# Two LayerNorms in a row folded into one, and input and output moved by groups, in a twelve-stage fp32 network on one core

## The reference, cut to what matters

```python
def _layernorm(x, axis=-1, eps=1e-05):
    m = jnp.mean(x, axis=axis, keepdims=True)
    v = jnp.var(x, axis=axis, keepdims=True)
    return (x - m) / jnp.sqrt(v + eps)
...
x = x + 0.5 * _L1_ffn_ref(_layernorm(x, axis=-1), L1_ffn_weight, L1_ffn_ln_gamma, L1_ffn_ln_beta)
...
x = x + _L3_attn_ref(_layernorm(x, axis=-1), ...)
...
def _L1_ffn_ref(x, weight, ln_gamma, ln_beta):     # ffn1, the quantised stage
    mu = jnp.mean(x, axis=-1, keepdims=True)
    var = jnp.var(x, axis=-1, keepdims=True)
    xn = (x - mu) * jax.lax.rsqrt(var + 1e-3) * ln_gamma + ln_beta
    ...
    gamma = jnp.max(jnp.abs(xn))                   # over all tokens: nothing goes on before all are normalised
    xq = jnp.clip(xn * QB / gamma, -QB + EPS, QB - EPS)
    y = jnp.einsum('bsd,du->bsu', xq, w_q)
    return y * (gamma * beta / QB)

def _L3_attn_ref(x, ...):                          # attn3, 16 heads, relative positions
    mu = jnp.mean(x, axis=-1, keepdims=True)
    var = jnp.mean((x - mu) ** 2, axis=-1, keepdims=True)
    xn = (x - mu) * jax.lax.rsqrt(var + 1e-05) * ln_gamma + ln_beta
    ...
```

## Time and profile before

| what | before |
|---|---|
| median of 3 runs | 4579.53 us (4579.15 to 4584.91) |
| span of the profiled execution | 4582.6 us |
| PE busy, share of the span | 3971.2 us, 87% |
| VectorE busy | 3493.0 us, 76% |
| ScalarE busy | 3069.3 us, 67% |
| GpSimd busy | 1526.0 us, 33% |
| mean granted TensorE clock | 0.928 of full |

### The profile page before, as it was taken

The page is one execution under the profiler, slowest core; times in us unless marked ns, Lnnn a source line. Parts: engine busy times, 40 slices in busy tenths (PEclk is TensorE's granted clock), DMA queues, the critical chain, the costliest instruction groups (busy, mean ns, idle before and its releaser), DMA issues.

```text
span 4582.6 us, 66148 instructions
## 1 busy us (share of the span) xinstructions
PE 3971.2 (87%) x15980; PEld 2219.1 (48%) x15980; DVE 3493.0 (76%) x11277; ACT 3069.3 (67%) x5649; POOL 1526.0 (33%) x2846
## 2 busy tenths in 40 slices
PE   5688759999999999999999999994878549999965
PEld 4466624444444444444444444442555437777744
DVE  5898479888888788887887887885656956666678
ACT  3455338999899899998998998992222216666632
POOL 2322124444444444444443443443000014333310
PEclk8888769999999999999999999996999769999977
DMA  2122010000000000100000000000000001111100
GB/s 56 29 34 37 15 23 1 1 24 1 15 10 1 20 6 1 25 1 15 10 1 20 6 1 22 3 1 0 1 0 0 1 14 43 43 43 43 43 1 18
DMA packets 151432, 71.88 MB, mean 16 GB/s; under 512 B 109433, under 2 KB 141902, under 8 KB 151012
## 3 DMA queue, kind: packets, MB, share of 16 engines
q1 hardware_dynamic: 144612, 64.16, 5.6%
q10 hardware_dynamic: 6400, 3.15, 0.2%
HBM read 54.48 MB, written 12.80 MB: 15 GB/s over the span
## 4 chain that ended last, share of the span: by engine, by line
PE 55%; DVE 21%; ACT 12%; issue 8%; DMA 1%; POOL 1%; DVEq 0%; ACTq 0%; SPq 0%; POOLq 0%
PE bank L1877 19%; PE bank L1892 6%; PE bank L1921 5%; PE bank L2663 5%; PE bank L1931 3%; DVE arena L1324 2%; PE bank L2696 2%; DVE arena L1328 2%; PE bank L655 2%; ACT arena L1969 2%; ACT arena L1968 2%; ACT L2015 2%; ACT arena L1981 2%; ACT arena L1972 2%; PE bank L2723 1%
## 5 line engine op out<-in xcount | busy, mean ns | idle before, releaser
L1877 PE MATMUL bank<-arena 128*128 128x512 f32 x3072 | 1423.2, 596 | 12.6 <-DVE arena L2058 6.1
L1877 PEld LDWEIGHTS bank<-arena 128*128 128x128 f32 x3072 | 587.2, 191 | 758.7 <-issue 730.1
L2118 POOL TENSOR_SCALAR arena<-arena 128x256 f32<-128x256 f32 x1024 | 483.7, 483 | 1191.0 <-DVE arena L2051 1191.0
L1892 PE MATMUL bank<-arena 128*128 128x512 f32 x1024 | 526.6, 606 | 64.8 <-DVE arena L2081 64.4
L2040 DVE SCALAR_TENSOR_TENSOR arena<-arena 128x256 f32<-128x256 f32 x1024 | 393.9, 421 | 185.9 <-ACT arena L1969 178.1
L2081 DVE SCALAR_TENSOR_TENSOR arena<-arena 128x256 f32<-128x256 f32 x1024 | 493.5, 526 | 13.5 <-issue 12.4
L2058 DVE SCALAR_TENSOR_TENSOR arena<-bank,bv,arena 128x256 f32<-128x256 f32 x1024 | 445.1, 472 | 0.0
L1968 ACT ACTIVATE arena<-bank,bqk 128x512 f32<-128x512 f32 x512 | 348.3, 680 | 81.5 <-PE bank L1877 72.9
L2051 DVE SCALAR_TENSOR_TENSOR arena<-bank,bq,arena 128x512 f32<-128x512 f32 x512 | 384.3, 751 | 18.0
L1981 ACT ACTIVATE arena<-arena,const_table 128x512 f32<-128x512 f32 x512 | 374.5, 731 | 0.0
L1972 ACT ACTIVATE arena<-bank,bqk 128x512 f32<-128x512 f32 x512 | 354.1, 692 | 0.7 <-PE bank L1877 0.6
(11 more groups left out here) (370 smaller groups left out, 7497.0 us busy)
## 6 DMA issues: line engine op xcount, KB each, us to landing
arena<-packed_dram SPq DMA_DIRECT2D x96, 96.0 KB
arena<-packed_dram SPq DMA_DIRECT2D x32, 288.0 KB
arena<-diag_dram SPq DMA_DIRECT2D x16, 256.0 KB, 4.0
arena<-in_L_attn_Wk_dram SPq DMA_DIRECT2D x16, 256.0 KB, 3.3
arena<-in_L_attn_Wq_dram SPq DMA_DIRECT2D x16, 256.0 KB, 4.0
arena<-in_L_attn_Wv_dram SPq DMA_DIRECT2D x16, 256.0 KB, 4.5
arena<-in_L_attn_Wo_dram SPq DMA_DIRECT2D x8, 512.0 KB, 3.9
arena<-in_L_attn_W_dram SPq DMA_DIRECT2D x16, 256.0 KB, 2.8
```

The lines of the kernel that those rows point to most:

```text
L1877: nc.tensor.matmul(bank[:, RING1[m % 5], :], w1p[k][:, i * P:(i + 1) * P], zT_of(g), start=True, stop=True).then_inc(a1_proj.sem, 1)
L1892: nc.tensor.matmul(bank[:, 6, :], wo1[:, i, :], a1_att[:, i % 4, :], start=(i == 0), stop=(i == NB1 - 1)).then_inc(a1_outd.sem, 1)
L2118: last = nc.gpsimd.tensor_scalar(a, a, 1.0, a1_ksum[:, i % 4, b:b + 1], ALU.add, ALU.mult)
```

## The change

It has three parts.

1. The second LayerNorm is folded into the first. With variance v and the two constants e1 and e2, the normalised x has mean 0 and variance v/(v+e1), so that both together are (x-m) / sqrt((1+e2)v + e1 e2). `ln_steps` takes the second constant (`again`), and `rstd_pool` multiplies by a slope and adds an offset in the one tensor_scalar where it added eps and multiplied by 1. `second_ln` with its four steps, and its tiles and semaphores, are gone.
2. In ffn1 VectorE's pipeline is stats (lag 0), apply (1), max (2). In attn3 the stats stand at w = 6, rstd at w = 7 on GpSimd, and apply at w = 10.
3. The first group of x is loaded by a transfer of its own that ScalarE issues as its first instruction (`group_loaded`), and SyncE's transfer brings the other seven; VectorE waits for these in the statistics of group 1. At the end SyncE waits for each group of the last stage and stores it by itself, 8 transfers of 256 KB.

```diff
-        def second_ln(n, eps, rep, apply_scale=None):
...
-        def ln_steps(n, eps, src=None):
+        def ln_steps(n, eps, again=None):
+            slope, offset = (1.0, eps) if again is None else (1.0 + again, eps * again)
...
             def stats_dve(g, u):
                 if n:
                     x_written.wait(nc.vector, t(g) - G)
+                elif isinstance(g, int) and g == 1:
+                    nc.vector.wait_ge(loaded, 16)
...
-                nc.gpsimd.tensor_scalar(rstd[:, u, :], meanvar[:, u, :, 1], eps, 1.0, ALU.add, ALU.mult)\
+                nc.gpsimd.tensor_scalar(rstd[:, u, :], meanvar[:, u, :, 1], slope, offset, ALU.mult, ALU.add)\
...
         def ffn1(n, rep):
-            stats_dve, rstd_pool, apply_dve, _, _ = ln_steps(n, 1e-5)
-            stats2_dve, rstd2_pool, apply2_dve, transpose_pe = second_ln(n, 1e-3, ln2_reps[0])
+            stats_dve, rstd_pool, apply_dve, transpose_pe, _ = ln_steps(n, 1e-5, 1e-3)
...
-                lambda e: over_groups(e, [(0, stats_dve), (1, apply_dve), (1, stats2_dve), (2, apply2_dve),
-                                          (3, max_dve)]),
+                lambda e: over_groups(e, [(0, stats_dve), (1, apply_dve), (2, max_dve)]),
...
-            programs["gpsimd"] += [lambda e: over_groups(e, [(0, rstd_pool), (1, rstd2_pool)]), scale_pool]
+            programs["gpsimd"] += [lambda e: over_groups(e, [(0, rstd_pool)]), scale_pool]
...
         def attn3(n, rep):
-            stats_dve, rstd_pool, apply_dve, _, _ = ln_steps(n, 1e-5)
-            stats2_dve, rstd2_pool, apply2_dve, transpose_pe = second_ln(n, 1e-5, ln2_reps[0])
+            stats_dve, rstd_pool, apply_dve, transpose_pe, _ = ln_steps(n, 1e-5, 1e-5)
...
-                for at, fn in ((4, stats_dve), (6, apply_dve), (8, stats2_dve), (11, apply2_dve)):
+                for at, fn in ((6, stats_dve), (10, apply_dve)):
...
-                if w == 5:
+                if w == 7:
                     pool.append((0, rstd_pool))
-                if w == 9:
-                    pool.append((0, rstd2_pool))
...
-                    sp.dma_start(x[:], A["L0_attn_x"].rearrange("b (k p) d -> p (b k) d", p=P)).then_inc(loaded, 16)
+                    sp.dma_start(x[:, QT:], tokens(A["L0_attn_x"])[:, QT:]).then_inc(loaded, 16)
...
-                x_written.wait(sp, len(stages) * G - 1)
-                sp.dma_start(out.rearrange("b (k p) d -> p (b k) d", p=P), x[:]).then_inc(stored, 16)
-                sp.wait_ge(stored, 16)
+                for g in range(G):
+                    x_written.wait(sp, (len(stages) - 1) * G + g)
+                    sp.dma_start(tokens(out)[:, g * QT:(g + 1) * QT], x[:, g * QT:(g + 1) * QT]).then_inc(stored, 16)
+                sp.wait_ge(stored, 16 * G)
...
-                dve.wait_ge(loaded, 16)
+                dve.wait_ge(group_loaded, 16)
...
             def _(act):
                 grant(act, "scalar")
+                act.dma_start(x[:, 0:QT], tokens(A["L0_attn_x"])[:, 0:QT]).then_inc(group_loaded, 16)
```

More of the change, by code:

```diff
@@ L225, in macaron, with tokens @@
         xT = sb("xT", [P, 2, NQ, 1 + T])
+        def tokens(a):
+            return a.rearrange("b (k p) d -> p (b k) d", p=P)
         def tiles(g):
@@ L236, in macaron @@
         loaded = sem("loaded")
+        group_loaded = sem("group_loaded")
         table_loaded = sem("table_loaded")
@@ L255, in apart @@
             eng.sem_inc(passed[eng.engine], 1)
-        def second_ln(n, eps, rep, apply_scale=None):
-            def stats_dve(g, u):
-                ln_applied.wait(nc.vector, g + n * G)
-                for q in range(QT):
-                    last = nc.vector.bn_stats(stats2[:, u, q, :], xn[:, u, q, :])
-                last.then_inc(ln2_stats.sem, 1)
-                ln2_stats.wait(nc.vector, g + rep * G, 1)
-                apart(nc.vector)
-                for q in range(QT):
-                    last = nc.vector.bn_aggr(meanvar2[:, u, q, :], stats2[:, u, q, :])
-                last.then_inc(ln2_stats.sem, 1)
-            def rstd_pool(g, u):
-                ln2_stats.wait(nc.gpsimd, g + rep * G)
-                apart(nc.gpsimd)
-                nc.gpsimd.tensor_scalar(rstd2[:, u, :], meanvar2[:, u, :, 1], eps, 1.0, ALU.add, ALU.mult)\
-                    .then_inc(ln2_rstd.sem, 1)
-                ln2_rstd.wait(nc.gpsimd, g + rep * G, 1)
-                nc.gpsimd.tensor_tensor(rstd2[:, u, :], rstd2[:, u, :], neghalf[:, 0:QT], ALU.pow)\
-                    .then_inc(ln2_rstd.sem, 1)
-            def apply_dve(g, u):
-                ln2_rstd.wait(nc.vector, g + rep * G)
-                xt_psum.wait_free(nc.vector, g + n * G)
-                for q in range(QT):
-                    last = nc.vector.tensor_scalar(zn[:, u, q, :], xn[:, u, q, :], meanvar2[:, u, q, 0:1],
-                                                   rstd2[:, u, q:q + 1], ALU.subtract, ALU.mult)
-                last.then_inc(ln2_applied.sem, 1)
-            def transpose_pe(g, u):
-                ln2_applied.wait(nc.tensor, g + rep * G)
-                xt_ready.wait_free(nc.tensor, g + n * G)
-                for q in range(QT):
-                    last = nc.tensor.transpose(bank[:, u, q * P:(q + 1) * P], zn[:, u, q, :], ident)
-                last.then_inc(xt_psum.sem, 1)
-            return stats_dve, rstd_pool, apply_dve, transpose_pe
-        def ln_steps(n, eps, src=None):
+        def ln_steps(n, eps, again=None):
+            slope, offset = (1.0, eps) if again is None else (1.0 + again, eps * again)
             def t(g):
@@ L446, in ffn0 @@
             programs["scalar"].append(lambda e: over_groups(e, [(0, copy_act), (1, act)], gate(e, n)))
-        if used & {"ffn1", "attn3"}:
-            stats2 = sb("stats2", [P, 2, QT, 6])
-            meanvar2 = sb("meanvar2", [P, 2, QT, 2])
-            rstd2 = sb("rstd2", [P, 2, QT])
-            zn = sb("zn", [P, 2, QT, D])
-            ln2_stats = ev("ln2_stats", per=2)
-            ln2_rstd = ev("ln2_rstd", per=2)
-            ln2_applied = ev("ln2_applied", credit=2, by="vector")
         if "ffn1" in used:
@@ L511, in ffn1 @@
         def ffn1(n, rep):
-            stats_dve, rstd_pool, apply_dve, _, _ = ln_steps(n, 1e-5)
-            stats2_dve, rstd2_pool, apply2_dve, transpose_pe = second_ln(n, 1e-3, ln2_reps[0])
-            ln2_reps[0] += 1
+            stats_dve, rstd_pool, apply_dve, transpose_pe, _ = ln_steps(n, 1e-5, 1e-3)
             def affine_act(g, u):
@@ L2907, in attn3 @@
             programs["scalar"].append(program_act)
-        ln2_reps = [0]
         emit = {"ffn0": ffn0, "ffn1": ffn1, "ffn2": ffn2, "ffn3": ffn3, "attn2": attn2, "attn3": attn3, "attn0": attn0, "attn1": attn1}
```

## The result

The changed kernel takes 4524.51 us, the median of 4 runs (4515.96 to 4534.13); the kernel before, beside it, 4579.34 us (4575.07 to 4584.91, 4 runs). The ratio is 0.9885, with a 95% interval of 0.9873 to 0.9896: 47.6 to 58.2 us less, 54.8 by the medians. The prediction was 4526.4 us.

What follows compares the result with a forecast made beforehand. VectorE was taken to bound ffn1's first phase, TensorE the long attention stages. Terms of 39.9 + 4.1 + 3.0 + 1.8 + 4.3 sum to 53.1 us: 4529.5 us profiled, forecast median 4526.4 us, range 4519 to 4541.

Steps and rivals of the forecast that it cites:

- ffn1: First phase of ffn1, twice: second statistics and apply leave VectorE's slot, one slot fewer; 39.9 us saved, bounds 37.4 to 41.1.
- The start of attn3: Start of attn3: TensorE takes the tiles after the first apply, not the second; 4.1 us saved, bounds 3.5 to 4.2.
- Within attn3: Seven attn3 halves with a LayerNorm: half its work goes; 3.0 us saved, the middle of 0 to 6.4.
- The input: Program start: group 0 lands by itself, so the first apply starts earlier; 1.8 us saved, bounds 0.8 to 2.8.
- If that rest lands at 12.4: Input step: with the rest of x landed at 12.4, the first apply starts at 13.7, 1.8 us earlier.
- less than 1 us: Input step: loss if the small transfer delays the table and first weights, covered by the wait.
- The output: Program end: only a last 256 KB store remains, tail 3.7 us; 4.3 us saved, bounds 3.5 to 5.3.
- (A): Rival at the program's ends: load and store changes give nothing; 47.0 us saved, 4532.5 us; chance 0.07.
- (B): Rival in ffn1: each apply waits for a GpSimd power, 16 us, 4543 us; chance 0.03.
- (C): Rival in attn3: apply at w = 10 stalls each half, 14 us lost, 4543 us; chance 0.03.
- (D): Rival in attn1: TensorE's clock is slowed; at 0.97 77 us are lost, 4603 us; chance 0.02.

Runs made afterwards that it cites:

- max_first: The changed kernel with VectorE's maximum put ahead of statistics and apply in each ffn1 slot: 4566.53 us in one run.
- attn3_alone: The kernel before with the folded LayerNorm and its new places in attn3 only: 4576.51 us (10 runs), ratio 0.9985 to the kernel before.
- io_only: The kernel before with group 0 of x loaded on ScalarE's queue and the eight stores, both LayerNorms kept: 4572.89 us (11 runs), ratio 0.9982.
- place_4_6: The changed kernel with attn3's statistics, factor and apply at the old places w = 4, 5 and 6: 4536.45 us in one run.

## Why the prediction was right, point by point

**ffn1, 39.9 us predicted, 41.3 measured.** The mechanism is as stated: VectorE is the bound in both kernels, its slot is what it has to do, and the way through TensorE and ScalarE stays covered. `max_first` shows that cover by taking it away. The size was off by 0.7 us a phase: the slot is 2.99 us in the mean (from the first apply's end, 4.03 us after the first statistics, to the last apply's start, 21.98 us after them, six slots) and not 3.09, which gives 0.6, and the tail is 4.02 us and not 4.1. That is the overlap that the text had put on top of its sum; the total lies just above the upper bound of 41.1.

**The start of attn3, 4.1 predicted, 4.9 measured,** 4.7 in `attn3_alone`. The removed step is the 4.07 us of the earlier trace rows, and the first work on queries and keys comes 4.1 us sooner in the changed kernel (16.88 against 20.97 us after the first statistics). What lies between that work and the first maximum varies by itself, from 20.1 to 21.0 us over all executions: the other kernels with the same work have 37.1 to 37.9 us for the whole start, and `io_only`, with both LayerNorms, has 41.4. So the 0.8 us above the forecast are not of the fold.

**Within attn3, 3.0 predicted, 6.2 measured,** some 5.3 of it by the usual lengths, inside the bounds of 0 to 6.4 but far from the middle that was taken. The usual half with the LayerNorm is 37.42 us, in the range of 37.2 to 38.1 that was named. The step that was mis-sized is the gain of a half: the forecast took 0.43 us (3.0 over 7), the usual half gives 0.68, and the first half, which the prediction took to be like the others, gives 1.2. What the prediction could not tell from the earlier trace rows, which piece costs what, `place_4_6` tells for the usual half: half the gain is the work, half is the place.

**The input, 1.8 predicted, 0.1 measured: this step failed,** and its lower bound of 0.8 with it. The failing sentence is "If that rest lands at 12.4"; in the changed kernel it lands at 14.14. The reason given, that the bytes in flight are the same, was not enough: the last of them land later when x is split, at 14.0 to 14.5 us in nine executions with it and at 12.5 to 13.3 in four with one transfer. By the means of these executions the load gives 0.5 us at the first apply, still under the lower bound. The loss of the first weights that the text allowed for is larger than its "less than 1 us", 1.75, and covered as it said.

**The output, 4.3 predicted, 5.4 measured.** The mechanism holds, the size was off: the last store takes 2.62 us from issue to the end and not 3.7, because the earlier trace rows had a store of another kind as the nearest row, 3.2 us, and this one lands in 2.2. The upper bound of 5.3 had been worked out from just that 2.2.
By the fit of the Trainium skill (DMA: Bandwidth & Descriptors, section Anatomy of one DMA) the estimate was 2.6 us for 256 KB: nearer than the row that was used, and still above the 2.2 that the trace shows.

**The sum.** 57.8 us by the stages, 53.1 predicted, 54.8 by the medians: an input that gave next to nothing was more than made up for by ffn1, attn3 and the store. The closeness of 4524.51 to 4526.4 is partly that cancelling, and partly luck: a median of this kernel moves by some us, 4524.51 and 4527.6 in two series.

**The rivals.** (A), ends that give nothing: right for the input, wrong for the store; together the ends give 5.5 of their 6.1. (B), VectorE and GpSimd holding each other up in ffn1: not there, the apply takes 1.08 to 1.11 us with the power beside it; with memsets beside it, in attn0, it does happen, before the change as after it. (C), a worse pipeline in attn3: no, the half is shorter; edges of the loop stay at 39 to 40 us in both kernels. (D), the clock: 1.00 in attn1, and attn1 is not longer.

## What to carry to other kernels

Before counting removed work as time, find what stands between the instruction that starts a round trip to other engines and the one that waits for its result: here 2.9 us of VectorE's own work against a trip of 2.3, and with the order changed the same kernel lost 35 of 41 us. Split a load so that the first consumer and the second are both served by early pieces; a first group by itself moves the wait to the second group (the first apply came at 15.45 us, and at 13.20 with more pieces, a gain that the total time does not tell). Read a long stage that the change doesn't touch in two executions of the same kernel before explaining a difference in it: here it moved by 13 us by itself, a quarter of the whole gain.

## What the runs showed of the hardware

- Four applies (128x128, fp32) took 1.11 us alone and 5.53 us beside GpSimd's memsets of 128x2048, in attn0; 5.46 us where an experiment put them beside memsets in attn3. Beside the power on 128x4 they took 1.08 to 1.11.
The Trainium skill (SBUF — State Buffer, section SBUF: two separate sides) calls the ports that the two share an exclusive lock, for some of VectorE's operations. The memset rows agree with it; the power's rows show no such delay.
- Eight stores of 256 KB landed in 2.2 us in the median, where stores of the same size within attn3 took 3.2.
- A load of 2 MB landed at 12.5 to 13.3 us of the program in one transfer (four executions) and at 14.0 to 14.5 in two or four (nine executions), with the DMA engines only partly busy at the end of either.
- attn1, some 2510 us at a granted clock of 1.00 in the stretch shown, took 2505.9 and 2518.8 us in two executions of one kernel.
